# Attention and feed-forward in one block: feed-forward tiles between the last attention steps, and the first scales made in the attention loop

## The reference

```python
x = layernorm(x + hyena(x))                    # FFT convolutions, 256 channels
x = layernorm(x + cross_attention(x, ctx))     # 16 heads of 16, 64 context rows per batch
# feed-forward with ternary weights and activations rounded to 8 bits
q(x)  = clip(round(x * s)) / s,  s = 127 / clip(max|x|) per row
wq(w) = clip(round(w / mean|w|), -1, 1) * mean|w|
hid = silu(q(x) @ wq(w_gate).T) * (q(x) @ wq(w_up).T)      # 1024 wide
x = layernorm(x + q(hid) @ wq(w_down).T)
```

## Time and profile before

| | us |
|---|---|
| three runs | 823.0, 826.8, 826.23 (median) |
| profiled execution, its own time | 830.26 |
| its span | 828.1 |
| first matmul of the attention loop to its last projection | 523.4 to 676.0 |
| first feed-forward matmul to the last hid's start | 685.0 to 808.7 |
| TensorE busy in the span | 702.4 (85%) |
| VectorE | 643.4 (78%) |
| ScalarE | 382.0 (46%) |
| GpSimd | 372.0 (45%) |

### The profile page before, as it was taken

How to read it: one execution, slowest core, us unless ns; L and a number is a source line. 1 busy time by engine, 2 the same in 40 slices (tenths; PEclk the granted TensorE clock), 3 DMA queues, 4 the chain that set the end, 5 groups by cost and what they waited for, 6 DMA issues and landing times. The chain is left out here.

```text
span 828.1 us, 12514 instructions
## 1 busy us (share of the span) xinstructions
PE 702.4 (85%) x4398; PEld 507.9 (61%) x4414; DVE 643.4 (78%) x1194; ACT 382.0 (46%) x701; POOL 372.0 (45%) x519
## 2 busy tenths in 40 slices
PE   3889998977989779987798988689999947888893
PEld 1378756866658566576676854477777732555552
DVE  2798778899888998789988751458888826899982
ACT  4432264301473113822126245656666634777773
POOL 0733425653148531485416512707423123476776
PEclk9999999989999899998999999789999996999998
DMA  8250055230052720527410557400000000000012
GB/s 292 80 102 1 0 136 119 51 51 0 7 95 55 179 21 1 102 51 144 73 52 25 137 143 258 149 2 2 2 2 2 2 0 2 1 27 27 33 45 76
DMA packets 37049, 52.79 MB, mean 64 GB/s; under 512 B 4761, under 2 KB 31386, under 8 KB 36732
## 3 DMA queue, kind: packets, MB, share of 16 engines
q0 software_dynamic: 7680, 16.77, 12.7%
q1 hardware_dynamic: 28604, 33.92, 12.3%
q10 hardware_dynamic: 704, 1.32, 0.6%
HBM read 31.04 MB, written 8.39 MB: 48 GB/s over the span
## 5 line engine op out<-in xcount | busy, mean ns | idle before, releaser
L644 ACT ACTIVATE yb<-banks 128x256 f32<-128x256 f32 x64 | 24.4, 385 | 230.2 <-PE banks L407 171.4
L398 PE MATMUL banks<-inv_m,spec_y 128*128 128x256 f32 x384 | 87.6, 381 | 8.0 <-POOL spec_y L765 8.0
L431 PE MATMUL banks<-xt_in,w_in 128*128 128x512 f32 x192 | 86.1, 604 | 3.3 <-DMA xt_in<-in_x_t 3.3
L398 PEld LDWEIGHTS banks<-inv_m,spec_y 128*128 128x128 f32 x384 | 72.3, 190 | 20.7 <-POOL spec_y L765 11.2
L355 PE MATMUL banks<-z_cplx,fwd_m 128*128 128x256 f32 x240 | 73.0, 386 | 10.5 <-DVE prod L989 7.5
L764 POOL TENSOR_TENSOR spec_y<-prod 128x256 f32<-128x256 f32 x64 | 49.2, 769 | 64.1 <-DVE prod L989 63.0
L356 PE MATMUL banks<-z_cplx,fwd_m 128*128 128x256 f32 x240 | 72.3, 383 | 0.0
L431 PEld LDWEIGHTS banks<-xt_in,w_in 128*128 128x128 f32 x192 | 37.0, 194 | 48.6 <-issue 48.4
L369 PE MATMUL banks<-z,fwd_m 128*128 128x256 f32 x168 | 46.0, 436 | 21.0 <-DVE sums_c L936 16.1
L355 PEld LDWEIGHTS banks<-z_cplx,fwd_m 128*128 128x128 f32 x240 | 45.5, 192 | 19.4 <-issue 9.7
L988 DVE TENSOR_TENSOR prod<-banks,spec_h 128x512 f32<-128x512 f32 x64 | 44.0, 687 | 15.5 <-POOL spec_y L765 6.5
(11 more groups left out here) (237 smaller groups left out, 1725.7 us busy)
## 6 DMA issues: line engine op xcount, KB each, us to landing
xt_in<-in_x_t SPq DMA_DIRECT2D x4, 1024.0 KB, 6.6
x_tok<-in_x SPq DMA_DIRECT2D x8, 512.0 KB, 4.3
x_tok<-in_b_out POOLq DMA_DIRECT2D x8, 512.0 KB, 13.2
x_scratch<-x_tok SPq DMA_DIRECT2D x8, 512.0 KB, 2.9
x<-x_scratch SPq DMA_DIRECT2D x8, 512.0 KB, 8.8
v_t<-left POOLq DMA_DIRECT2D x8, 511.5 KB, 5.5
x_t<-left POOLq DMA_DIRECT2D x8, 511.5 KB, 5.0
out<-x SPq DMA_DIRECT2D x7, 512.0 KB, 2.9
```

Source lines behind the costliest of these rows:

```text
L398: last = mm(bank[:, odd * 2 * P:(odd + 1) * 2 * P], spec_y[:, j + odd, part * D + h * P:part * D + (h + 1) * P], inv_m[:, o:o + 2 * P], st ...
L431: last = mm(proj_pair(b, t)[:, c * 512:(c + 1) * 512], w_in[:, k, TILES[t] * P:(TILES[t] + 1) * P], xt_in[:, k, c * 512:(c + 1) * 512], st ...
```

## The change

`attention` and `feed_forward` become one function with one block, so that no engine drains between them. The steps of feed-forward are the same, with new names (`turn_x` is `turn_input`, `evac_x` `evac_input`, `square` `square_out`, its `add_residual` `add_down`, its `norm_factors` `out_factors`, `norm` `normalize_out`); what changes is where they stand in the queues, and the memory. The matmul outputs of feed-forward now share the banks of attention: gate and up lie in those of the scores, both transposes in those of turn_prob, down in those of the context and the inverses. hid lies over the raw weights. x_peak, x_unit and x_scale have a column for each tile, so `x_scales` waits for no earlier user. `norm_last` is gone; GpSimd normalizes the last chunk after its step 2.

```diff
+X_LATE, X_EARLY = 22, 2
...
+        hid = w_raw[:].rearrange("p i n -> p (i n)")[:, 0:CH * INNER].rearrange("p (k n) -> p k n", k=CH)
...
+        ps_gate, ps_up = ps_score[:, 0:INNER], ps_score[:, INNER:2 * INNER]
+        ps_xt, ps_ht = ps_pt[:, 0:512].bitcast(BF16), ps_pt[:, 512:1024].bitcast(BF16)
+        ps_down = (ps_ctx, ps_inv)
@@ tensor, after the attention loop @@
+            pe.wait_ge(ident_ready, 1)
+            pe.wait_ge(pt_evac, TILES_ALL)
+            turn_input(0)
             project(HALVES - 2)
             sums(HALVES - 1)
+            pe.wait_ge(shifted, TILES_ALL)
+            pe.wait_ge(w_seq, 9)
+            inner(0, ps_gate, w_gate, silu_done, gate_mm)
+            turn_input(1)
             spread_inverses(HALVES - 1)
             values(HALVES - 1)
-            project(HALVES - 1)
+            inner(0, ps_up, w_up, h_ready, up_mm)
+            for s in range(TILES_ALL + 3):
+                if s + 1 in tiles:
+                    inner(s + 1, ps_gate, w_gate, silu_done, gate_mm)
+                if s == 0:
+                    project(HALVES - 1)
+                if s - 3 in tiles:
+                    if s == 3:
+                        pe.wait_ge(added, HALVES)
+                    down(s - 3)
+                if s - 2 in tiles:
+                    turn_hidden(s - 2)
+                if s + 2 in tiles:
+                    turn_input(s + 2)
+                if s + 1 in tiles:
+                    inner(s + 1, ps_up, w_up, h_ready, up_mm)
@@ scalar, after the attention loop @@
+            evac_input(0)
             squares(HALVES - 3)
+            gate(0)
+            evac_input(1)
             evac_inverses(HALVES - 1)
             squares(HALVES - 2)
-            squares(HALVES - 1)
-            norm_last(CHUNKS - 1)
+            for s in range(TILES_ALL + 4):
+                if s + 1 in tiles:
+                    gate(s + 1)
+                if s == 0:
+                    squares(HALVES - 1)
+                if s - 2 in tiles:
+                    evac_hidden(s - 2)
+                if s + 2 in tiles:
+                    evac_input(s + 2)
+                if s - 4 in tiles:
+                    square_out(s - 4)
@@ gpsimd, after the quantization @@
-            for c in range(2, CHUNKS - 1):
+            for c in range(2, CHUNKS - 2):
                 norm_chunk(c)
-            norm_factors(CHUNKS - 1)
+            round_x(0)
+            round_x(1)
+            back_scales(0)
+            norm_chunk(CHUNKS - 2)
+            round_x(2)
+            for s in range(TILES_ALL):
+                back_hidden(s)
+                round_hidden(s)
+                if s % CH == 1 and s // CH + 1 < CHUNKS:
+                    back_scales(s // CH + 1)
+                if s + 3 in tiles:
+                    round_x(s + 3)
+                if s == 2:
+                    norm_chunk(CHUNKS - 1)
...
@@ vector @@
             nc.vector.memset(v_pairs[:], 0.0).then_inc(v_zero, 1)
+            nc.vector.tensor_copy(ident_b[:], ident[:]).then_inc(ident_ready, 1)
...
+            def x_peaks(c):
+                dve.wait_ge(x2_ready, c + 1)
+                reduce(x_peak[:, c * CH:(c + 1) * CH], x2[:, c * CH:(c + 1) * CH, :], AX_X, ALU.max,
+                       apply_absolute_value=True).then_inc(x_peaked, 1)
+
+            def x_scales(c):
+                of = slice(c * CH, (c + 1) * CH)
+                dve.wait_ge(x_peaked, c + 1)
+                ts(x_unit[:, of], x_peak[:, of], CLIP, 1.0 / QMAX, ALU.max, ALU.mult).then_inc(x_floored, 1)
+                dve.wait_ge(x_floored, c + 1)
+                recip(x_scale[:, of], x_unit[:, of]).then_inc(x_scaled, 1)
...
             for j in range(TILES_ALL):
                 shift(j)
...
                 elif i >= 1:
                     normalize(i - 1)
+                c, late = divmod(j - X_LATE, CH)
+                if late == 0 and c in range(X_EARLY):
+                    x_peaks(c)
+                if late == 1 and c in range(X_EARLY):
+                    x_scales(c)
             normalize(HALVES - 2)
             add_residual(HALVES - 2)
             invert(HALVES - 1)
             normalize(HALVES - 1)
-            add_residual(HALVES - 1)
+            dve.wait_ge(w_seq, 9)
+            for s in range(TILES_ALL + 3):
+                if s in tiles:
+                    hidden(s)
+                if s == 0:
+                    add_residual(HALVES - 1)
+                if s - 3 in tiles:
+                    add_down(s - 3)
+                if s in tiles:
+                    floor_peak(s)
+                    hidden_scale(s)
+                c = s // CH + X_EARLY
+                if s % CH == 1 and c < CHUNKS:
+                    x_peaks(c)
+                    x_scales(c)
```

More of the change, by code:

```diff
@@ L1358, in project, with low_halves, turn_input, inner @@
                 last.then_inc(wo_mm, 1)
+            def low_halves(rows):
+                return rows.bitcast(BF16).rearrange("p (n two) -> p n two", two=2)[:, :, 0]
+            def turn_input(i):
+                pe.wait_ge(x_rounded, i + 1)
+                if i:
+                    pe.wait_ge(input_evac, i)
+                for t in range(DT):
+                    last = transpose(ps_xt[:, t * P:(t + 1) * P], low_halves(xq_f[:, i % 2, t * P:(t + 1) * P]), ident_b[:])
+                last.then_inc(input_mm, 1)
+            def inner(i, ps, w, free, done):
+                pe.wait_ge(input_evac, i + 1)
+                if i:
+                    pe.wait_ge(free, i)
+                for n in range(2):
+                    for t in range(DT):
+                        last = mm(ps[:, n * HALF:(n + 1) * HALF], xq_t[:, i % 2, t, :], w[:, t, n * HALF:(n + 1) * HALF],
+                                  start=(t == 0), stop=(t == DT - 1))
+                last.then_inc(done, 1)
+            def turn_hidden(i):
+                pe.wait_ge(h_rounded, i + 1)
+                if i:
+                    pe.wait_ge(ht_evac, i)
+                for t in range(FT):
+                    last = transpose(ps_ht[:, t * P:(t + 1) * P], low_halves(hid[:, i % CH, t * P:(t + 1) * P]), ident_b[:])
+                last.then_inc(ht_mm, 1)
+            def down(i):
+                pe.wait_ge(ht_evac, i + 1)
+                if i >= 2:
+                    pe.wait_ge(f_added, i - 1)
+                for t in range(FT):
+                    last = mm(ps_down[i % 2][:, 0:D], hq_t[:, i % 2, t, :], w_down[:, t, :],
+                              start=(t == 0), stop=(t == FT - 1))
+                last.then_inc(down_mm, 1)
             scores(0)
@@ L1452, in squares, with evac_input, gate, evac_hidden @@
                        accum_out=row_var[:, c % 2, k:k + 1]).then_inc(squared, 1)
[L1454 to L1458, removed]
+            def evac_input(i):
+                act.wait_ge(input_mm, i + 1)
+                if i >= 2:
+                    act.wait_ge(up_mm, i - 1)
+                fn(xq_t[:, i % 2].rearrange("p t n -> p (t n)"), ps_xt[:, 0:D].bitcast(I16), ACT.Copy).then_inc(input_evac, 1)
+            def gate(i):
+                act.wait_ge(back, 2 * (i // CH + 1))
+                act.wait_ge(gate_mm, i + 1)
+                if i >= 2:
+                    act.wait_ge(h_ready, i - 1)
+                fn(silu[:, i % 2, :], ps_gate[:], ACT.Silu, scale=gate_back[:, i // CH % 2, i % CH:i % CH + 1])\
+                    .then_inc(silu_done, 1)
+            def evac_hidden(i):
+                act.wait_ge(ht_mm, i + 1)
+                if i >= 2:
+                    act.wait_ge(down_mm, i - 1)
+                fn(hq_t[:, i % 2].rearrange("p t n -> p (t n)"), ps_ht[:].bitcast(I16), ACT.Copy).then_inc(ht_evac, 1)
+            def square_out(i):
+                act.wait_ge(f_added, i + 1)
+                c, k = i // CH, i % CH
+                if i:
+                    act.wait_ge(f_squared, i)
+                if c >= 2:
+                    act.wait_ge(f_floored, c - 1)
+                fn(f_spread_sq[:], x2[:, i, :], ACT.Square, scale=-float(D), bias=f_row_sum[:, c % 2, k:k + 1],
+                   accum_out=f_row_var[:, c % 2, k:k + 1]).then_inc(f_squared, 1)
             for j in range(TILES_ALL):
@@ new lines, in round_hidden, with back_hidden @@
+            def round_hidden(i):
+                pool.wait_ge(h_scaled, i + 1)
+                k = i % CH
+                ts(hid[:, k, :], hid[:, k, :], h_scale[:, k:k + 1], MAGIC, ALU.mult, ALU.add).then_inc(h_rounded, 1)
+            def back_hidden(i):
+                pool.wait_ge(h_floored, i + 1)
+                if i >= CH:
+                    pool.wait_ge(f_added, i - CH + 1)
+                k = i % CH
+                tt(down_back[:, k:k + 1], h_unit[:, k:k + 1], w_mean[:, 2:3], ALU.mult).then_inc(back_down, 1)
@@ L1586, in add_residual @@
                 last.then_inc(added, 1)
[L1588 to L1601, removed]
```

340 lines of the change are left out of this document (103 added, 237 removed).

## The result

The changed kernel took 812.77 us (median of 4 runs, 812.0 to 813.11) beside 826.51 us for the kernel before on the same chip (4 runs, 823.0 to 828.65): a ratio of 0.9834, 95% interval 0.9807 to 0.986. Forecast were 811.7 us. The profiled run took 812.0 us, its span is 809.3.

What follows compares the result with a forecast made beforehand. TensorE bounds the attention loop; TensorE, ScalarE and VectorE race closely in feed-forward, with an 8.95 us TensorE hole between. Handover -15.4, ramp -0.4 and loop +1.3 sum to -14.5 us: 811.7 us from the 826.23 median, range 808.5 to 817.

Steps and rivals of the forecast that it cites:

- Handover, -15.4: From attention's end to hid(0): the first tile waits for no attention result, gate(0) fills a TensorE gap; 15.4 us less.
- the switch holds more: Rival at ScalarE's table load: idleness before it hides a hold, up to 2.03 us, total up to 813.7; chance 0.04.
- Loop, +1.3: Attention loop: x_peaks and x_scales of two chunks inserted on VectorE cost 0.65 us each, bounds 0.7 to 3.2 for both.
- two turns 0.65 late: Sign of being right, in the attention loop: two turns each delayed 0.65 us by the inserted scale work.
- Ramp, -0.4: hid(0) to hid(5): 19.75 us instead of 20.18, GpSimd's last chunk taking back nearly all the full-clock gain.
- the stall at hid(5) by GpSimd's last chunk: In the ramp: GpSimd's 4.08 us chunk delays tile 6's rounding, so up(5) and hid(5) slip about 1.85 us.
- nothing of the step depends on that: Profiled execution 4.0 us above the median: claimed irrelevant to the change, so the gain was taken off the median, 826.23.
- From hid(5) the queues are those of before, so I give the rest nothing: From hid(5) onward, the remaining feed-forward tiles: same queues as before, so no change in time.
- Clock falls in the ramp: Rival in the ramp: sparse TensorE work lowers its clock, 1.9 us per dip, 813.6 to 815.5 us; chance 0.22.
- Tiles start too late: Rival: gate(0) misses its gap, hid(0) 4.5 us later, or the loop pays its upper cost; 813.6 to 816.2; chance 0.13.
- half clock stays: Rival: interleaved TensorE stays at half clock, 3.2 us per tile; 0.03 for within 0.5%, 0.03 for slower.
- The GpSimd chunk is hidden: Rival in the ramp: other slowness covers up to 1.85 us of the GpSimd stall, total 809.9 us; chance 0.04.

Runs made afterwards that it cites:

- no_interleave: Changed kernel with every attention step ahead of the first feed-forward step on TensorE, ScalarE and VectorE; 819.7 us, ratio 0.9912 to the kernel before.
- early_table: Changed kernel with ScalarE loading the silu table behind squares(13), before it waits for gate(0); 813.59 us, ratio 0.9847 to the kernel before.
- scales_after_loop: Changed kernel with x_peaks and x_scales of chunks 0 and 1 moved from the attention loop to behind it; 811.38 us, ratio 0.9814.
- spread_chunk7: Changed kernel with GpSimd's last-chunk factors in step 3 and its four normalizations spread over steps 4 to 7; 811.42 us, ratio 0.9818.
- old_waits: Changed kernel with the two removed, long fulfilled waits put back in x_scales of chunks 2 to 7; 814.08 us, ratio 0.9839.
- squares_later: Changed kernel with ScalarE evacuating transposed tile 2 ahead of attention's last squares; 812.06 us, ratio 0.9841 to the kernel before.

## Why the prediction was right, and where it was not

- **Handover, -15.4: right**, by its own steps: measured -15.53 between the same instructions. gate(0) fits the gap, hid(0) follows the normalization, and no_interleave shows that 7.4 us of it are the interleaving. The rule of the Trainium skill (ScalarE: Activation LUTs, section What ACT_TABLE_LOAD costs) of 1.38 us of drain beside the load, which would have made the gain smaller, doesn't show: the load took 1.28 and the silu began at once, here, in no_interleave and in early_table, where the load stood directly behind the squares. The rival that the switch holds more falls with it.
- **Loop, +1.3: the mechanism was right, the term mis-sized**: 0.70. I took about 0.95 of VectorE's 1.25 us of waiting as lying behind the insertion; scales_after_loop gives 1.61 - 0.35 = 1.26, all of it. The lower bound was the value, and of my sign "two turns 0.65 late" the stages show 0.35.
- **Ramp, -0.4: right against the profile that I had, but off by 2.9 us against the second.** Its parts held: the wait behind the squares (1.70, expected 1.8), the stall at hid(5) by GpSimd's last chunk (1.6 by spread_chunk7; I wrote 1.85, where my own two times, 693.4 and 691.8, give 1.6). That the changed ramp met 19.75 to 0.01 is luck: hid(3) to hid(4) took 3.69 for 3.25, since the squares delay up(4) after all, and hid(4) to hid(5) 5.35 for 5.65. What failed is that of the profiled execution being 4.0 us above the median "nothing of the step depends on that": the step did depend on it: 2.9 us of the profile's length were a clock that its ramp had lost for longer than the second profile's did. By the second profile the same ramp is +2.45.
- **"From hid(5) the queues are those of before, so I give the rest nothing": wrong**, -1.3. The change takes two waits off x_scales; I knew that and gave it no price, and didn't read x_unit's durations in the profile of before, 0.17 in some chunks and 1.04 in others. old_waits, with the two waits back, has 98.15 again.
- **The sum.** Against the second profile of before, the errors are -0.1 in the handover, -0.6 in the loop, -1.35 in the rest and +2.85 in the ramp, together +0.8: -13.7 instead of -14.5. The total came out within 1.1 us because errors of up to 2.9 us cancelled; that is luck.
- **Clock falls in the ramp: did not come**, but in squares_later it did, after an edit that moves 0.5 us. My price for a dip, 1.9, was somewhat high: it cost 1.6 there, and 1.7 in the kernel before (hid(3) to hid(5), 8.36 in the first profile and 6.70 in the second). My reading that a sparse three microseconds brings it did not hold: no_interleave had 0.87 and 0.62 of 3 at full clock. **Tiles start too late, half clock stays: refuted** by hid(0) and by 1.00 throughout. **The GpSimd chunk is hidden: refuted**, spread_chunk7 gives 1.6 us back in the ramp, of which 0.6 are lost again by hid(9).

Why the clock of the kernel before comes back 3.6 us after TensorE's first transpose in one profile (683.93 to about 687.5) and 10 us after it in the other (684.97 to about 695) is open; nothing here was run for it.

## What to carry to other kernels

Between two phases, look for what the first tile of the second really needs: here about half of the handover's gain was not the overlap but that the first tile's inputs no longer depended on the last normalizations, the drain and scales made after them, and an early input costs little where its engine waits anyway (price it by all the waiting the engine has, then check that with the stages). A removed wait in a diff is a change of phase, and where VectorE and GpSimd meet, a tenth of a microsecond made an operation nine tenths longer; what of it reached the end was 1.3 us over five chunks. A stall that is taken away shows the next bound: here TensorE and ScalarE, every 3.75 us, took back 0.6 of 1.6. Cut spans at the same instructions and take a second profile of the old kernel before crediting a stage in which its clock was low.

## What the hardware showed that I had not expected

- A 128x4 operation of VectorE in SBUF took 0.10 to 0.19 us alone and up to 1.04 us (before, first profile) where a 1.12 us operation of GpSimd had begun before it; the reciprocal on the same tile, right behind it, took 0.18 in each case, also at 711.89 in the changed kernel, where GpSimd's operation ran until 712.78.
- TensorE's clock fell to 1.2 GHz behind a stretch with 0.87 of 3 us busy (squares_later) and behind one with 1.16 of 3, and stayed at 2.4 GHz behind one with 1.25 of 3 in the changed kernel and behind two with 0.87 and 0.62 of 3 in no_interleave. The busy share doesn't tell these cases apart.
- Two waits on VectorE that are already fulfilled put about 0.1 us between an operation and the next: x_peak ends at 714.31 and x_unit starts at 714.44 in old_waits; in the changed kernel these are 711.64 and 711.67.
